# Attention stage on one core: the scores of two units issued together, ahead of the transposes of each odd unit

## The reference, cut to what matters

```python
# layer 2: qkv in one product, mask where adj == 0, then a layernorm of the result
attn = softmax(where(adj == 0, -inf, q @ k.T * scale)); o = (attn @ v) @ w_proj + b_proj; return o + ln(o)
# layer 3: separate Wq, Wk, Wv, Wo with biases; masked by adding (1 - adj) * -1e9
attn = softmax(q @ k.T / sqrt(32) + (1 - adj) * -1e9); return (attn @ v) @ Wo + bo
```

## Time and profile before

| what | us |
|---|---|
| median of three runs | 3034.55 |
| profiled execution, its own time | 3033.56 |
| span of the profile | 3031.7 |
| TensorE matmul busy in the span | 2927.1 (97%) |
| VectorE busy | 2402.1 (79%) |
| ScalarE busy | 2124.1 (70%) |
| mean granted TensorE clock | 0.986 |

### The profile page before, as it was taken

One profiled execution on the slowest core, in us unless ns is written; L12 is line 12 of the kernel. 1 busy time (PEld: TensorE's weight loads), 2 busy tenths in 40 slices (PEclk: granted clock), 3 DMA queues, 4 the chain that ended last, 5 costly groups with the idle time before them and its releaser, 6 DMA issues.

```text
span 3031.7 us, 64907 instructions
## 1 busy us (share of the span) xinstructions
PE 2927.1 (97%) x23872; PEld 2207.6 (73%) x23872; DVE 2402.1 (79%) x4427; ACT 2124.1 (70%) x3794; POOL 590.8 (19%) x538
## 2 busy tenths in 40 slices
PE   7999997999999999999999989999999999999998
PEld 6888886777676767777677767776767676767776
DVE  6776675879797978888888888887878787878886
ACT  3000003888787878878788878887888787878887
POOL 2222220105050504041322333010101010102000
PEclk9999999999999999999999999999999999999999
DMA  3101104233232332332323252323232332323232
GB/s 122 35 22 57 42 15 106 57 81 74 61 93 56 84 71 67 78 78 64 90 54 95 71 133 64 91 64 91 64 83 67 73 74 62 94 54 88 67 74 57
DMA packets 123647, 217.86 MB, mean 72 GB/s; under 512 B 20016, under 2 KB 88240, under 8 KB 123312
## 3 DMA queue, kind: packets, MB, share of 16 engines
q1 hardware_dynamic: 122160, 209.14, 28.1%
q0 software_dynamic: 1152, 4.19, 0.5%
HBM read 53.87 MB, written 25.17 MB: 26 GB/s over the span
## 4 chain that ended last, share of the span: by engine, by line
PE 78%; issue 2%; ACT 2%; DVE 1%; DMA 0%; DVEq 0%; POOL 0%; ACTq 0%; POOLq 0%
PE t_pt_ps L740 31%; PE t_ot_ps L759 17%; PE t_s_ps L728 15%; PE t_g_ps L713 4%; PE t_g_ps L714 4%; PE t_g_ps L715 4%; PE t_g_ps L780 1%; PE t_g_ps L784 1%; ACT t_T L878 1%; PE t_g_ps L799 1%; ACT t_PT L883 1%; DVE t_st_lo L965 0%; DMA mask<-in_adj 0%; ACT t_st_hi L868 0%; ACT t_ot L889 0%
## 5 line engine op out<-in xcount | busy, mean ns | idle before, releaser
L947 DVE CUSTOM_DVE_ANT_0 t_T<-t_s_ps,mask 128x1024 f32<-128x1024 f32 x1024 | 1240.7, 1215 | 180.8 <-PE t_s_ps L728 180.8
L878 ACT ACTIVATE t_T<-t_T,t_low 128x1024 f32<-128x1024 f32 x1024 | 1178.8, 1151 | 57.2 <-DVE t_low L947 38.4
L740 PEld LDWEIGHTS t_pt_ps<-t_ident,t_T 128*128 128x128 f32 x8192 | 889.0, 142 | 329.6 <-issue 281.6
L740 PE MATMUL t_pt_ps<-t_ident,t_T 128*128 128x128 f32 x8192 | 1116.2, 279 | 6.8 <-DVE t_PT L1022 4.7
L883 ACT ACTIVATE t_PT<-t_pt_ps 128x512 f32<-128x512 f32 x1324 | 756.0, 596 | 367.1 <-PE t_pt_ps L740 357.4
L728 PE MATMUL t_s_ps<-t_k,t_q 128*128 128x512 f32 x2048 | 735.2, 440 | 46.6 <-issue 39.5
L1022 DVE COPY t_PT<-t_pt_ps 128x512 f32<-128x512 f32 x724 | 498.8, 689 | 199.1 <-PE t_pt_ps L740 195.5
L759 PE MATMUL t_ot_ps<-t_PT,shared 128*32 128x256 f32 x8192 | 556.9, 390 | 8.1 <-ACT t_PT L883 7.8
L759 PEld LDWEIGHTS t_ot_ps<-t_PT,shared 128*32 128x32 f32 x8192 | 215.9, 110 | 261.0 <-issue 138.2
L728 PEld LDWEIGHTS t_s_ps<-t_k,t_q 128*128 128x128 f32 x2048 | 313.2, 193 | 49.9 <-issue 43.4
L255 ACT ACTIVATE g_yT_hi<-g_ps 128x512 fp32r<-128x512 f32 x64 | 38.3, 598 | 402.0 <-PE g_ps L195 402.0
(11 more groups left out here) (185 smaller groups left out, 3156.4 us busy)
## 6 DMA issues: line engine op xcount, KB each, us to landing
t_q<-t_st_hi SPq DMA_DIRECT2D x256, 128.0 KB, 2.3
t_k<-t_st_hi SPq DMA_DIRECT2D x256, 128.0 KB, 2.4
t_k<-t_st_lo SPq DMA_DIRECT2D x256, 128.0 KB, 2.4
t_q<-t_st_lo SPq DMA_DIRECT2D x256, 128.0 KB, 2.4
shared<-x_after_graph_layers SPq DMA_DIRECT2D x8, 1024.0 KB, 7.3
t_xe<-x_after_graph_layers SPq DMA_DIRECT2D x32, 256.0 KB, 3.6
x_after_layer<-t_xe SPq DMA_DIRECT2D x32, 256.0 KB, 2.2
shared<-x_after_layer SPq DMA_DIRECT2D x8, 1024.0 KB, 7.3
```

The lines of the kernel that those rows point to most:

```text
L740: last = nc.tensor.transpose(pt_ps[half][:, i * P:(i + 1) * P], T[u % RING][:, kt * P:(kt + 1) * P], ident[:])
L878: nc.scalar.activation(T[u % RING][:], T[u % RING][:], ACT.Exp, bias=low[:, u % RING:u % RING + 1], scale=-1.0, accum_out=rsum[:, u:u + 1] ...
L947: nc.vector.tensor_tensor_reduce(out=T[u % RING][:], in0=s_ps[u % 2][:], in1=mask[:, qt, :], scale=1.0, scalar=3.4e38, op0=ALU.add, op1=AL ...
```

## The change

An odd unit u issues S(u+2) where it did, at its start, and then S(u+3) just before its own T(u). An even unit issues no scores. Ahead of the first job S(2) is issued too. S(u+3) waits for M(u+1), as S of that unit did before; only its place in TensorE's program differs. The order of all other work, on all engines, is the same. In a pair of an odd unit u and the even unit u+1 the program was S(u+2), block, T(u), S(u+3), block, V, T(u+1), and is S(u+2), block, S(u+3), T(u), block, V, T(u+1).

```diff
                 for u in range(UNITS):
-                    if u + 2 < UNITS or after is not None:
+                    if u % 2 and (u + 2 < UNITS or after is not None):
                         scores(job, u + 2, UNITS * job + u + 1)
...
                         for w in range(u, u + GROUP):
                             values(job, w)
+                    if u % 2 and (u + 3 < UNITS or after is not None):
+
+                        scores(job, u + 3, UNITS * job + u + 2)
                     transposes(job, u)
...
             scores(0, 1, None)
+            scores(0, 2, 1)
```

## The result

The changed kernel takes 3016.84 us (median of 4 runs, 3013.46 to 3018.04) against 3034.12 us of the kernel before in the same comparison: ratio 0.994, 95% interval 0.9923 to 0.9958. The prediction was 3021 us, range 3001 to 3036. The profiled execution took 3017.47 us, span 3015.7, 16.0 less than the span before.

A forecast was written before the change was run, and what follows sets the result against it. TensorE, 97% busy, was taken as the bound. Jobs 1 to 14 give 9.4 us, job 0 0.4, job 15 about 1.2, boundaries 2.6: 13.6 us, so 3021 us against the median, range 3001 to 3036.

The forecast's parts named there:

- The wait in the plain pair: T(odd) without a block waits for copies C0, C1 of the even unit; 0.10 us saved in 16 units, 1.60 a job.
- Entering V, and odd units with a block: Entering V costs the same from T or S; 13 odd units with a block go 2.42 to 2.40, taken as nothing.
- Unit 7: V of unit 8 waits for C0(7), behind the `ot_ps` copy on ScalarE, so V stays where it is: gain 0.
- V of unit 16: V needs C0(15) and can start 1.29 after T(15); TensorE, ready at 0.97, waits 0.32 us.
- Units 37 to 40: Unit 37's later block finish delays M(40), then S(42), E(40), the `ot_ps` copy, C0(39) and V of 40: cost 0.48 us.
- The 0.13 one pair earlier: Same late chain at units 35 to 37, with a block in the way that gives 0.36: cost 0.13 us.
- Job ends: Next job's scores move ahead of the loop back: gain 0.35 at ten, loss 0.17 at five other boundaries, together 2.6 us.
- The stop itself unchanged: At the ten loop backs TensorE's stop of 3.87 us was taken to stay the same.
- at most 1 us: In job 7, T(61) is delayed behind S(64), which waits for late DMAs of head 0: at most 1 us, once.
- wait for M(u+1): Rival, chance 0.10: S(u+3) waits for M(u+1) in plain pairs, holding T(odd) behind it; 11 us slower, 3046.
- The slack of 0.20: In plain pairs M(u+1)'s signal comes 2.93 behind T(odd) and S(u+3) wants it at 3.13: the smallest slack, 0.20 us.
- T behind scores costs 0.10 by itself: Rival, chance 0.05: a drain going from scores into T; 13 block units lose 0.10 each, 2.2 a job in all, 3065.

The follow-up runs named there:

- shorter copies: Kernel before, old order, but C0 and C1 copy only 256 of their 512 columns, leaving out part of the transposed probabilities: 2992.09 us, ratio 0.9856.
- the block units alone: Kernel before, with the new order only in the 13 odd units that have a block: 3050.47 us, ratio 1.0045.
- the run without 37: Changed kernel, but units 15 and 37 keep the old order: 3005.70 us, ratio 0.9903.
- the edit alone: Kernel before, with only S(2) of the next job moved ahead of T(63), so before the loop back: 3027.52 us, ratio 0.9973.
- the kernels with the plain units: Kernel before, new order only in the 18 odd units without a block other than 39: 3000.57 us; with first `ot_ps` copy on VectorE too: 2998.87 us.

## Why the prediction was right, step by step

- **The wait in the plain pair.** Right in mechanism: shorter copies take the same 0.10 away that the new order takes. The size was read a little high: 0.10 in units 2 to 4, but 0.07 to 0.09 in most pairs whose even unit has a block (20, 22, 26, 28, 30, 42, 54). Per job, the 15 pairs give 1.36 by their medians and the first pair another 0.1 where the clock was full on both sides, against 1.60.
- **Entering V, and odd units with a block: nothing.** Right. T to V is 0.96 and V to T 1.00 in the trace after; the run with the block units alone shows them at 0.00. The drain at a change of tiling mode, which the Trainium skill states in TensorEngine Tiling (Array Packing), Key Properties, agrees: what V costs on entry stayed the same when its neighbour became T instead of S.
- **Unit 7: nothing.** Right (pair from 6: 0.00), and for the reason given: with the copy of `ot_ps` off ScalarE it is 0.30 shorter.
- **V of unit 16: 0.32.** Measured 0.31; gone when unit 15 keeps the old order.
- **Units 37 to 40: 0.48.** Measured 0.47, by the chain M(40), E(40), copy, C0(39), V. The step before it misled: the visible wait of S(42) for M(40), which the prediction put first, costs nothing beside that chain. Taking that wait away left the whole 0.47. The 0.13 one pair earlier did not show (0.00); unit 35's lateness is real but appears only in the run without 37, as 0.25 at unit 40 and 0.07 in the pair from 36.
- **Job ends: mis-sized.** 2.6 us predicted, 8.1 measured by themselves (5.2 to 11.2 by the ratio's interval). The term had two sizes in it, and both were off. The gross gain at a loop back was priced at 0.73; the trace of the edit alone has 1.30. What the slow clock takes back was priced at a half of it, 0.37; that trace has 0.58, and the two traces of the changed kernel 0.49 and 0.11. Net it is 0.72 each, just the upper bound of 0.73. "The stop itself unchanged" did not hold: "issue" in front of the first matmul behind it sums to 39.5 us before and 39.8 with the block units alone, but to 36.7 and 35.1 in the changed kernel and 35.0 with this edit alone, so 0.28 to 0.45 of each stop goes too. The run with shorter copies has the old order and 35.3, so it is not the place of the scores alone that does it; why, no run here shows.
- **The clock behind the loop backs, overlooked.** How long the clock stays at 0.50 there is not the same from run to run. Over the ten loop backs these stretches last 54.6 us in the trace before, 44.4 and 41.0 in the two of the changed kernel, 47.8 with the edit of job ends alone and 64.9 with the block units alone, the run that was 3 us slower than its pairs. Two kernels that differ by one copy of `ot_ps` far from the job's end have 27.3 and 47.8, and need 125.9 and 131.9 us from T(62) to T(2). A part of what the job ends gave is therefore not the order's doing, and which part was not separated.
- **DMAs at the change of layer.** S(64) of job 7 waited 4.4 us for the DMA of its k, with T(61) behind it, and the pair from 60 was 1.27 longer there, close to the "at most 1 us"; in the kernels with the plain units it was 0.5 to 3.9. The pairs from 62 and 0 behind it give most of that back, so that the three together are between 1.3 shorter and 2.8 longer than before. Waits for the loads of the new mask stand beside it (4.9 us on VectorE); which of the two sets the time was not tested.
- **The rivals.** Plain pairs do not wait for M(u+1): in the trace after, the third score matmul of a plain unit starts more than 0.3 us behind the second only at unit 39 (15 of 15 jobs), in the slow stretch behind loop backs and at the start of job 0, and at the change of layer. The slack of 0.20 held: in units 2 to 4 the last row of M(4) ends at 1451.07, 0.23 ahead of the weight load of that third matmul. That T behind scores costs 0.10 by itself is excluded by the 11 block units at 0.00 and by the shorter copies.

The sum, 13.6 us, fell short of the 16.1 between the two profiled executions (17.3 between the medians). That it came so near is in part luck: the plain pairs gave some 2 us less than priced, the missing 0.13 gave 2 back, and the job ends gave more than the prediction had a reason for.

## What to carry to other kernels

When two engines hand one buffer back and forth, moving independent work between the two uses hides the hand-over, but it also makes the second use later; look for who waits for that one by a deadline of its own. A wait shown in the profile is not the price: price the chain that ends at the next common point, and check it by taking the wait away. An order that pays in one kind of step need not be used in all: here it earns 20 us in the plain units and can only delay in the 13 units with a block, and two of those (15 and 37) cost 12 us.

## What the runs showed of the hardware

- Four or eight 128x128 fp32 transposes follow a 512-column fp32r matmul without any gap: 0.23 us from start to start, as between two equal score matmuls. Entering the 32-column tiles of V loses 0.09 to 0.10 us from either kind. Leaving them loses some too: eight transposes need 0.85 us to the next start behind V and 0.80 behind scores.
- From the start of a T behind V to the next T that overwrites its buffer it is 1.43 us, with ScalarE's copy over 0.14 ahead of it; from a T behind scores to a V that reads the copy 1.29 us. ScalarE's copy of 128x512 out of PSUM took 0.60 us, VectorE's 0.69.
- A loop back stopped TensorE for 3.5 to 4.0 us on the average of the ten (34.8 to 39.8 us in all, by trace), 4.4 at most, and its granted clock was at 0.50, the 1.2 GHz level, behind it for part or all of the first V and often of T(0) too; how far it reached differs from job to job and run to run, and single traces differ by some us for it.
